# Attention kernel: chains of key differences four pairs long in place of two, and a narrower row of maxima

## The reference, cut to what matters

```python
h = group_norm1(x, n1_g, n1_b)
f = dwconv(h, w3, b3) + dwconv(h, w5, b5) + dwconv(h, w7, b7)
g = jax.nn.sigmoid(conv1x1(f, gate_w, gate_b))
x = x + conv1x1(f * g, proj_w, proj_b)
h = group_norm1(x, n2_g, n2_b)
q = conv1x1(h, q_w, q_b).reshape(B, C, N).transpose(0, 2, 1)
k = conv1x1(h, k_w, k_b).reshape(B, C, N)
v = conv1x1(h, v_w, v_b).reshape(B, C, N).transpose(0, 2, 1)
attn = jax.nn.softmax(jnp.einsum('bnc,bcm->bnm', q, k) * C ** -0.5, axis=-1)
out = jnp.einsum('bnm,bmc->bnc', attn, v)
return x + out.transpose(0, 2, 1).reshape(B, C, H, W)
```

## Time and profile before

| | |
|---|---|
| median of 3 runs | 2643.19 us (2640.99 to 2645.05) |
| profiled execution, its own time | 2642.42 us |
| its span, first to last instruction | 2640.7 us |
| granted TensorE clock over the span | 0.995 |
| busy share: PE, POOL, ACT, DVE | 97%, 84%, 82%, 75% |
| chain that ended last, by engine | PE 84%, ACT 6%, issue 4%, DVE 3% |
| attention blocks of the first image | from about 163 us to 1345 us |

### The profile page before, as it was taken

One profiled execution on the slowest core, in us unless ns is written; L12 is line 12 of the kernel. 1 busy time (PEld: TensorE's weight loads), 2 busy tenths in 40 slices (PEclk: granted clock), 3 DMA queues, 4 the chain that ended last, 5 costly groups with the idle time before them and its releaser, 6 DMA issues.

```text
span 2640.7 us, 82914 instructions
## 1 busy us (share of the span) xinstructions
PE 2552.4 (97%) x34700; PEld 1426.2 (54%) x34700; DVE 1972.6 (75%) x3096; ACT 2176.7 (82%) x2198; POOL 2213.9 (84%) x1563
## 2 busy tenths in 40 slices
PE   7899999999999999999988999999999999999998
PEld 4356555555555555555434655555555555555553
DVE  5587777777777777777558777777777777777764
ACT  4478888888888888888867888888888888888887
POOL 1458989999899999999865799999999999999996
PEclk9999999999999999999999999999999999999999
DMA  6238888888888888888601788888888888888881
GB/s 207 54 73 170 182 182 182 182 182 182 182 181 183 183 181 182 182 182 184 135 6 37 149 179 177 177 177 177 179 179 179 179 178 178 179 174 180 179 168 29
DMA packets 144867, 424.43 MB, mean 161 GB/s; under 512 B 20072, under 2 KB 46184, under 8 KB 144112
## 3 DMA queue, kind: packets, MB, share of 16 engines
q0 software_dynamic: 107712, 374.39, 69.4%
q1 hardware_dynamic: 36784, 44.75, 6.1%
HBM read 16.41 MB, written 9.44 MB: 10 GB/s over the span
## 4 chain that ended last, share of the span: by engine, by line
PE 84%; ACT 6%; issue 4%; DVE 3%; POOL 2%; DMA 1%; ACTq 0%; POOLq 0%; SPq 0%; DVEq 0%
PE ps L1168 38%; PE ps L1157 31%; PE ps L1177 10%; ACT arena L691 4%; DVE mxp L950 2%; PE ps L1327 2%; POOL arena L527 1%; PE ps L1236 1%; ACT negm L722 1%; PE ps L1221 1%; PE ps L1355 1%; PE ps L1370 1%; ACT ps L738 1%; DMA accD<-arena 1%; PE ps L1415 0%
## 5 line engine op out<-in xcount | busy, mean ns | idle before, releaser
L958 DVE TENSOR_REDUCE mxp<-ps 128x1 f32<-128x512 f32 x2448 | 1689.1, 691 | 499.3 <-PE ps L1177 403.4
L691 ACT ACTIVATE arena<-ps,bnd 128x1024 f32<-128x1024 f32 x1296 | 1431.0, 1107 | 262.0 <-PE ps L1157 239.1
L527 POOL TENSOR_TENSOR arena<-arena 128x1024 f32<-128x1024 f32 x576 | 1549.7, 2690 | 107.1 <-ACT arena L691 99.9
L1168 PE MATMUL ps<-arena,vals 64*64 64x512 f32 x10368 | 1521.5, 590 | 0.0
L1177 PE MATMUL ps<-arena,QM 64*64 64x512 f16 x5184 | 987.7, 378 | 15.9 <-DVE mxp L950 8.9
L1157 PE MATMUL ps<-arena 64*64 64x512 f16 x10368 | 853.8, 378 | 21.3 <-ACT ps L738 6.2
L546 POOL DMA_DIRECT2D accD<-arena x544 | 647.6, 1190 | 3.0 <-DMA accD<-arena 1.8
L1168 PEld LDWEIGHTS ps<-arena,vals 64*64 64x64 f32 x10368 | 544.3, 133 | 145.4 <-issue 9.8
L738 ACT ACTIVATE ps<-arena 128x1024 f32<-128x1024 f16 x542 | 557.3, 1028 | 50.5 <-ACT arena L691 1.1
L1157 PEld LDWEIGHTS ps<-arena 64*64 64x64 f16 x10368 | 352.0, 106 | 436.6 <-issue 295.1
L1157 PE MATMUL ps<-arena,KD 64*64 64x512 f16 x5184 | 547.7, 376 | 0.3
(11 more groups left out here) (138 smaller groups left out, 888.9 us busy)
## 6 DMA issues: line engine op xcount, KB each, us to landing
accD<-arena POOLq DMA_DIRECT2D x612, 512.0 KB, 5.5
accD<-accD POOLq DMA_DIRECT2D x34, 512.0 KB, 6.9
arena<-arena POOLq DMA_DIRECT2D x68, 256.0 KB, 6.4
arena<-accD POOLq DMA_DIRECT2D x34, 512.0 KB, 8.8
arena<-arena SPq DMA_DIRECT2D x216, 64.0 KB, 2.5
arena<-in_x_rows SPq DMA_DIRECT2D x8, 816.0 KB, 9.8
f_scratch<-arena SPq DMA_DIRECT2D x32, 144.0 KB
f<-f_scratch SPq DMA_DIRECT2D x16, 288.0 KB, 4.7
```

The source lines that it names most:

```text
L527: nc.gpsimd.tensor_tensor(accA[:, n % 2, :], accA[:, n % 2, :], E[:, 0, at:at + 2, :].rearrange("p s c -> p (s c)"), ALU.add).then_inc(add ...
L691: nc.scalar.activation(E[:, :, slot_of(n, p), :], ps[:, S_BANK + 2 * buf:S_BANK + 2 * buf + 2, :], ACT.Exp, scale=bnd[:, 6:7]).then_inc(e_ ...
L958: nc.vector.reduce_max(flat(mxp[:])[:, 2 * v + t:2 * v + t + 1], ps[:, MX_BANK + t, :], AX.X).then_inc(mx_free, 1)
L1168: a = nc.tensor.matmul(ps[C * t:C * t + C, ACC_BANK + r, :], V[rows, p, t, :], E[rows, t, slot_of(n, p), :], start=(p == 0), stop=(p == NP ...
```

## The change

Pairs by difference become those with p % 8 not in (0, 3), from pair 4 on, so a run of pairs in one set of banks is a seed and three differences. Per image seeded pairs are 8, 11, 16, 19, 27, 32, 35 (and 24 in the first block). Every chunk of keys now has a difference in each column that needs one: GpSimd makes them in two pieces of 256 columns (one in the first chunk) into new columns TD beside T, signals them after its own chunk, and the parts KD and KL of odd chunks cover all 512 columns. The low part of the keys that are not differences is made only in even chunks. `negm` is 64 columns for each of its four parts in place of 128, and `widen_maxima` stands ahead of `seed` at p = 33.

```diff
-DIFF = CH // 2
+CHAIN = 8
...
-        KD = sb("KD", [P, NCH * DIFF], F16)
+        KD = sb("KD", [P, (NCH // 2 + 1) * 2 * P + NCH // 2 * CH], F16)
...
-        negm = sb("negm", [P, NQT, P], F16)
+        negm = sb("negm", [P, NQT, C], F16)
...
+        TD = E[:, 0, 4:8, :]
...
-            return p in (2, 3) or p >= GP and p % GP in (1, 2)
+            return p in (2, 3) or p >= GP and p % CHAIN not in (0, 3)
...
         def difference_cols(chunk):
 
+            if chunk % 2:
+                return slice(0, CH)
             return slice(2 * P, 4 * P) if chunk == 0 else slice(P, 3 * P)
+
+        def kd_cols(chunk):
+
+            first = chunk // 2 * (2 * P + CH) + chunk % 2 * 2 * P
+            at = difference_cols(chunk)
+            return slice(first, first + at.stop - at.start)
...
                     if chunk:
-                        difference(c, 1, c - 1, 3)
-                    if chunk == 1:
-                        difference(c - 1, 3, c - 1, 1).then_inc(diff_ready, 1)
-                    a = difference(c, 2, c, 0)
-                    if chunk:
-                        a.then_inc(diff_ready, 1)
...
+                        nc.gpsimd.tensor_tensor(TD[:, c % 4, lower], T[:, c % 4, lower], T[:, (c - 1) % 4, upper], ALU.subtract)
+                    nc.gpsimd.tensor_tensor(TD[:, c % 4, upper], T[:, c % 4, upper], T[:, c % 4, lower], ALU.subtract
+                                            ).then_inc(diff_ready, 1)
+                    if chunk % 2 == 0:
+                        by_pair = "p (k i) -> p k i"
...
-                nc.scalar.activation(negm[:], m4[:].unsqueeze(2).to_broadcast([P, NQT, P]), ACT.Copy, scale=-M_ROW
+                nc.scalar.activation(negm[:], m4[:].unsqueeze(2).to_broadcast([P, NQT, C]), ACT.Copy, scale=-M_ROW
...
                     if p == RESTART - 1 and j:
                         copy_row_sums(n - 1, S_BANK)
+                    if p == NPAIR - 3 and j + 1 < NBLK:
+                        widen_maxima(n + 1)
                     if p + 2 < NPAIR and is_seeded(j, p + 2):
                         seed(b, j, p + 2)
...
-                    if p == NPAIR - 3 and j + 1 < NBLK:
-                        widen_maxima(n + 1)
...
-                            nc.scalar.activation(KD[:, before[1] * DIFF:(before[1] + 1) * DIFF], T[:, (i - 1) % 4, difference_cols(before[1])], ACT.Copy
+                            nc.scalar.activation(KD[:, kd_cols(before[1])], TD[:, (i - 1) % 4, difference_cols(before[1])], ACT.Copy
```

More of the change, by code:

```diff
@@ L628, in low_of_queries @@
                     nc.gpsimd.tensor_tensor(QL[:, cols], T[:, c % 4, :], QH[:, cols], ALU.subtract).then_inc(lo_ready, 1)
-                def difference(c, at, of_c, of):
-                    return nc.gpsimd.tensor_tensor(T[:, c % 4, at * P:(at + 1) * P], T[:, c % 4, at * P:(at + 1) * P],
-                                                   T[:, of_c % 4, of * P:(of + 1) * P], ALU.subtract)
                 def keys_and_differences(c, chunk):
                     n = 2 * NCH * b + c
+                    lower, upper = slice(0, 2 * P), slice(2 * P, CH)
                     pool.wait_ge(t_ready, n + 1)
@@ L640, in keys_and_differences @@
                     if chunk:
-                        difference(c, 1, c - 1, 3)
-                    if chunk == 1:
-                        difference(c - 1, 3, c - 1, 1).then_inc(diff_ready, 1)
-                    a = difference(c, 2, c, 0)
-                    if chunk:
-                        a.then_inc(diff_ready, 1)
[L647 to L651, removed]
+                        nc.gpsimd.tensor_tensor(TD[:, c % 4, lower], T[:, c % 4, lower], T[:, (c - 1) % 4, upper], ALU.subtract)
[3 more added lines that the diff above has]
+                        by_pair = "p (k i) -> p k i"
+                        own = slice(0, 2) if chunk == 0 else slice(0, 4, 3)
+                        cols = slice(chunk * CH, (chunk + 1) * CH)
+                        nc.gpsimd.tensor_tensor(KL[:, cols].rearrange(by_pair, k=GP)[:, own, :],
+                                                T[:, c % 4, :].rearrange(by_pair, k=GP)[:, own, :],
+                                                KH[:, cols].rearrange(by_pair, k=GP)[:, own, :], ALU.subtract)
                 def low_of_differences(c, chunk):
@@ L657, in low_of_differences @@
                     pool.wait_ge(dh_ready, NCH * b + chunk + 1)
-                    nc.gpsimd.tensor_tensor(KL[:, cols], T[:, c % 4, at], KD[:, chunk * DIFF:(chunk + 1) * DIFF], ALU.subtract
-                                            ).then_inc(lo_ready, 1)
+                    nc.gpsimd.tensor_tensor(KL[:, cols], TD[:, c % 4, at], KD[:, kd_cols(chunk)], ALU.subtract).then_inc(lo_ready, 1)
                 for c, (which, chunk) in enumerate(QK_CHUNKS):
@@ L1145, in scores @@
                 if by_difference(p):
-                    at = p // GP * DIFF + p % GP * P - difference_cols(p // GP).start
+                    at = kd_cols(p // GP).start + p % GP * P - difference_cols(p // GP).start
                     of_hi, hi = KD, slice(at, at + P)
@@ L1198, in spread_maxima @@
                         for h in (0, 1):
-                            a = nc.tensor.matmul(ps[C * h:C * h + C, S_BANK + r, q * C:(q + 1) * C], negm[rows, q, 0:C],
+                            a = nc.tensor.matmul(ps[C * h:C * h + C, S_BANK + r, q * C:(q + 1) * C], negm[rows, q, :],
                                                  ident16[rows, rows], start=True, stop=True)
```

## The result

The kernel after the change takes 2566.88 us (median of 4 runs, 2564.03 to 2574.71); the kernel before takes 2644.12 us (4 runs, 2640.99 to 2645.13). The ratio is 0.9715, with a 95% interval of 0.9691 to 0.9738: 2.9% faster. The profiled execution has a span of 2562.3 us at a granted clock of 0.996, against 2640.7 us at 0.995. That is 78.4 us less span, where the forecast had 67.4. The profiled execution was the fastest of the four; by the medians the gain is 77.2 us.

The account below looks back on a forecast made before the run. PE was taken to set the middle blocks' pace, stalling on late second seeds from ScalarE. Terms 49.9 + 3.2 + 6.4 + 0 + 10.4 - 2.5 = 67.4 us gave a span of 2573.3 and 2575 us; range 2562 to 2594, up to 2606 with a rival.

Parts of the forecast that it names:

- term 3: End of block: narrower, earlier row of maxima lets exp 34 end 0.2 us sooner; gain 6.4 us, bounds -5 to +8.
- term 4: First block of each image: 1.0 us gained, but the moved row holds the seed of 35; taken as nothing, 2 us either way.
- term 6: Key preparation: wider GpSimd differences cost more, 2.5 us lost in the second image, nothing in the first; 7 without cover.
- 1 seeds: Middle blocks: six late second seeds of 0.26 us vanish, 1.56 us a block, 49.9 us in all; bounds 42 to 54.
- 2 row sums: Pair 22: its exp no longer waits behind the seed of 23, so PE's row sums start sooner; gain 3.2 us.
- 5 last blocks: Last block of each image, without looks: one lone seed per four pairs; gain 10.4 us for two blocks, 8 to 13.
- PE has no more to give: Rival, middle blocks: PE meets another wait whenever a seed is in time; about 2633 us; chance 0.08.
- GpSimd and the dumps take the pace: Rival: GpSimd's adds and dumps become the bound; 2600 us if half of the 50 us went there; chance 0.13.
- The reduction comes late: Rival: VectorE falls behind by pair 31, so the moved row holds seed 35, exp 34 and spreading; 2683 at 3 us; chance 0.05.

Follow-up runs that it names:

- work_waits: Kernel after, with an unread seed-sized activation per removed seed in the second image, each waiting for the exp ahead: 2590.71 us, one run; blocks there 65.30.
- last_pair: Kernel after, with pair 35 also taken by difference, so no seed stands behind the row of maxima: 2564.58 us, ratio to before 0.9712; middle block 64.01.
- row_late: Kernel after, with the narrow row of maxima put back behind the seed of pair 35: 2571.26 us, ratio to before 0.9720; middle block 64.38.
- move_only: Kernel before, with the row of maxima at full width moved ahead of the seed of pair 35: 2643.66 us, one run; middle block 66.29.
- prep_and_row: Kernel after, with the old pattern of seeds, keeping the wider key preparation and new row: 2638.50 us, ratio to before 0.9984; middle block 66.10.
- pool_64: Kernel after, with one more unread 64-column GpSimd add behind each dump: 2638.47 us, one run; middle blocks about 67.2, then 66.2.
- work_for_seeds: Kernel after, with an unread seed-sized activation for each removed seed in the second image, not waiting for the exp ahead: 2575.77 us, ratio to before 0.9746.

## Why the prediction was right

The forecast said 2575 us with a span of 2573.3; the kernel took 2566.88 with a span of 2562.3. It was faster, inside the range of 2562 to 2606 but close to its fast end, and 11 us of span better than the sum. (That range isn't quite the sum of the bounds given with the terms: with -5 for term 3, -2 for term 4 and 7 lost in term 6 the slow end of the forecast alone would be 2607 and not 2594.) By the sum's own terms, in us over the kernel:

| term | forecast | measured | from |
|---|---|---|---|
| 1 seeds | -49.9 | -49.9 | 1.56 x 32 |
| 2 row sums | -3.2 | -5.4 | 0.17 x 32 |
| 3 row of maxima | -6.4 | -12.5 | 0.39 x 32 |
| 4 first blocks | 0 | -2.0 | see below |
| 5 last blocks | -10.4 | about -10 | see below |
| 6 key preparation | +2.5 | +2.0 | second image |
| not in the sum | | about -0.5 | gates, start, longer blocks |
| span | -67.4 | -78.4 | |

1. *Seeds.* Right in place, number and size. Six late seeds of 0.26 are 1.56 us; the middle blocks lost 2.12 in all, of which 0.17 and 0.39 are booked under terms 2 and 3, which leaves 1.56. Directly, from exp 4 to exp 20 it is 27.55 us in place of 28.57, and from exp 24 to exp 32 13.77 in place of 14.29: 1.54. work_waits showed the mechanism: three late seeds cost three times 0.26, with ScalarE equally full. The rival that PE has no more to give is refuted by the 13 pairs at 1.72. By busy share there were 0.53 us in 60 to be had, and 3.2% came. The Trainium skill (Perfetto Trace Analysis, Identifying the Most-Contended Engine), by which matmul occupancy says little of how near the limit is, holds after the change too: the kernel after shows 64.00 of 64.00 us of PE busy from 700 to 764 us, and last_pair still took 0.20 off a block.

2. *Row sums.* This step of the prediction failed, and the gain in its place is luck. I took it that the row sums wait for exp 22, which stood behind the seed of 23, and set as its sign that they would start 0.2 after the look. They start 0.33 after it in both kernels (669.63 to 669.96 in the earlier trace rows; 719.78 to 720.11 here, where L1179 is the look and L1238 the row sums), and exp 22 had ended 0.26 us before them then and 0.53 now. So they never waited for it. PE at pair 23, in the kernel before, in the kernel after, and in the kernel after in one of its three blocks of 64.48 or 64.49:

```profile
668.98 0.84 PE L1157 MATMUL ps<-arena 64*64 64x512 f16 x12
...
719.14 0.58 PE L1159 MATMUL ps<-arena,KD 64*64 64x512 f16 x4
...
719.57 0.58 PE L1159 MATMUL ps<-arena,KD 64*64 64x512 f16 x4
719.78 0.40 PE L1179 MATMUL ps<-arena,QM 64*64 64x512 f16 x2
720.11 0.65 PE L1238 MATMUL ps<-arena,ones 128*64 128x256 f32 x4
...
654.92 0.41 PE L1159 MATMUL ps<-arena,KD 64*64 64x512 f16 x4
...
655.35 0.41 PE L1159 MATMUL ps<-arena,KD 64*64 64x512 f16 x4
```

The records of the twelve score matmuls run over 0.84 us in the first (668.98 to 669.82) and over 1.01 in the second (719.14 to 720.15), though pairs follow each other in 1.72 in both. The exp starts 0.04 or 0.05 behind the last of them, so exp 23 comes 0.17 later after the scores' start, and exp 24 doesn't: it follows that start by 4.20 us in both. That is why exp 23 to exp 24 went from 3.30 to 3.13. The three longer blocks decide what does it. In each one seed came 0.28 us late ahead of pair 23, and they show 0.84 (654.92 to 655.76) and 3.31 again, with no seed ahead of exp 22. So the short form is what PE's scores have once PE has stood and waited for a seed, and the 0.17 is a further price of the late seeds: 1.73 a block with it. Why PE's starts lie closer behind a wait isn't shown.

3. *Row of maxima.* This is the mis-sized term, 6.1 of the 11 us. The width gave 0.23 a block, as said (0.2). I gave the place nothing, because by the earlier trace rows the last reduction ended when exp 33 did, and took that distance as fixed. It isn't: it shrank by 0.16 us when term 1 took the stalls away, since exp 33 now starts later behind its scores, as exp 23 does. In the kernel after the place is worth 0.17 (row_late); in the kernel before it is 0.04 (move_only). Of the 0.39 a block 0.14, or 4.5 us of the kernel, comes only when both changes are made, and could be booked under term 1 as well. That scores of 35 would come 0.13 late was right: they start 1.86 after the scores ahead of them (677.12 less 675.26), 0.14 over the pace, and last_pair, which takes that seed away, gets 0.20 back.

4. *First blocks.* Right in kind, with the second part put too high. The 1.0 came: from exp 5 to exp 33 such a block takes 51.81 us in place of 52.87. And the row did hold the seed of 35: its reduction starts 2.10 us after exp 33 here, and exp 34 now comes 3.63 after exp 33, where it was 2.94 and is 2.91 in row_late. But nearly all of that is made good by the next pair. From exp 5 of the first block to exp 5 of the next it is 67.73 in the kernel after and 67.48 in row_late, so the row's earlier place costs 0.25 us in each first block and not the 1.0 that I set against the gain. Before it was 68.59, and 68.88 in the second image, where one seed came 0.28 late.

5. *Last blocks.* From the row to the load of the gate's table the last block of the first image takes 64.56 in place of 68.85. The row stands 0.75 earlier in it, so the block itself gained 5.0, and 5.2 were forecast. From exp 5 to exp 21 it takes 25.12 (1266.03 to 1291.15) in place of 27.71, 12.56 for eight pairs where 12.54 was the forecast's.

6. *Key preparation.* GpSimd's differences take 724 ns (L646, L647), where I had estimated 0.69 from two widths. In the second image 49.19 became 51.20 from the normalized form to the row: 2.0 in place of 2.5, and 2.2 in prep_and_row. In the first image nothing, as said.

The gate's stage of the second image differs by 1 to 1.5 us between traces whatever the kernel: ScalarE's idle time ahead of its fourth ACTIVATE was 3.42, 3.70, 2.01, 2.27, 3.57 and 2.28 in six of them. Between the two kernels it is 3.42 and 2.27, 1.15 us that no term explains.

*GpSimd and the dumps take the pace* didn't happen: one gap of an exp was 0.24 us longer than usual. The rival was weighed on the right margin. pool_64 puts a number to it: 1.3 to 3.1 us a block, and the change used 2.1. *The reduction comes late* didn't happen in the middle blocks, where it came 0.16 earlier against exp 33; in the two first blocks it did, at 0.25 us each (term 4). VectorE's pace between pairs 24 and 31 held (its reductions and reciprocals follow each other without idle time at 1.72 a pair), and row_late, which has no wait of the row ahead of the seed, is slower and not faster there, so that wait costs nothing.

## What to carry to other kernels

Compare starts of like groups, not busy time: an engine at 99% busy gave back 3%, because its records covered its waits. When work is taken off a full engine, ask who waits for it, since the same work cost 0.26 us in one place of the queue and nothing in the next. And a stall removed early in a cycle moves the others' work too: price each later part of a change against the cycle as it will be, or run it alone and together, as here 0.04 became 0.17. And look for the sign that a forecast named even when the sum comes out: 0.17 us came where 0.1 was forecast, and the wait that was to give it had never been there.

## What the runs showed of the hardware

An ACTIVATE that doesn't depend on the one ahead starts 0.10 us before that one's end (1.01 start to start behind an exp of 1.11); one that waits for it starts 0.09 after its end (1.20). The Trainium skill (ScalarE: Activation LUTs, What ACT_TABLE_LOAD costs) says that back-to-back ACTIVATEs overlap by about 93 ns, and the first of these agrees. The second, 0.19 us dearer, is the case of every seed here, and it decided the size of work_for_seeds.

The twelve 64x512 score matmuls of a pair are recorded over 0.84 us from a wait of PE for a seed up to the next pair with sixteen, and over 1.01 where PE hasn't waited since such a pair, at the same 1.72 us from pair to pair. The exp that reads them starts 0.17 later in the second case, so a distance measured from such a reader shifts by 0.17 when a stall goes.

The duration of a GpSimd instruction swells when DMA issues follow on it without a pause: between 700 and 730 us of pool_64 the same 1024-column add is recorded at 2.35 to 4.22 us, and the issue behind it, where it need not wait, starts 2.29 or 2.30 us after it. What it costs the queue is read from the starts. An add of 64 columns costs 0.24 us of queue and one of 128 columns 0.36, while the profile gives means of 1207 and 1425 ns for them. So the rise of the add's mean from 2690 to 2873 ns is by itself no sign of slower work. It goes with shorter pauses: 45.0 us of idle time ahead of the adds in place of 107.1.
